# A decoder layer on one core: the mixture's base product moved ahead of the router's end, the last chunk's cross-attention in a list of its own, the experts' product transposed, and a bias added on GpSimd

## What is computed

```
x = LN(x + L0(x))          h = x + mamba(rms(x));  L0 = h + silu(rms(h) W1) * (rms(h) W2) W3
x = LN(x + xattn(x, ctx))  16 heads, 64 keys; the scores are scaled a second time by a
                           temperature made from their mean, max and entropy by a small MLP
x = LN(x + ffn(x))         x W + b + sum over e of gate[e] * (x A[e]) B[e]
                           gate: softmax over 8 experts, the top 2 kept and renormalised
```

## Time and profile before

| | |
|---|---|
| median of 3 runs | 4170.89 us (4154.61 to 4172.75) |
| the profiled execution | 4160.77 us |
| its span, first to last instruction | 4159.0 us |
| TensorE busy (matmuls) | 3674.8 us, 88% |
| DVE / ScalarE / GpSimd busy | 2519.4 / 2165.4 / 2441.5 us, 61 / 52 / 59% |
| mean granted TensorE clock | 0.938 of 2.4 GHz |
| moved by DMA | 483 MB, 116 GB/s on the mean |
| chain of work that ended last | TensorE 58%, GpSimd 7%, ScalarE 6%, DVE 6% |

### The profile page before, as it was taken

The page is one execution under the profiler, slowest core; times in us unless marked ns, Lnnn a source line. Parts: engine busy times, 40 slices in busy tenths (PEclk is TensorE's granted clock), DMA queues, the critical chain, the costliest instruction groups (busy, mean ns, idle before and its releaser), DMA issues.

```text
span 4159.0 us, 36287 instructions
## 1 busy us (share of the span) xinstructions
PE 3674.8 (88%) x9984; PEld 1760.8 (42%) x9984; DVE 2519.4 (61%) x3286; ACT 2165.4 (52%) x5182; POOL 2441.5 (59%) x1069
## 2 busy tenths in 40 slices
PE   7667998899879999999989998999989998999477
PEld 3223443444334445544434345554334434554244
DVE  4884678567746886168755887158774787222211
ACT  5543544554555455565456547455466457340543
POOL 3884599559954995049963997029981998100000
PEclk9889999899989999999989999999989999999788
DMA  4433344335433442235433442125432443112000
GB/s 171 138 121 101 120 164 162 97 115 167 149 106 117 158 156 74 86 112 168 152 111 104 157 159 97 66 83 187 152 128 82 157 162 119 49 46 91 11 31 21
DMA packets 221268, 483.19 MB, mean 116 GB/s; under 512 B 31884, under 2 KB 32268, under 8 KB 220812
## 3 DMA queue, kind: packets, MB, share of 16 engines
q1 hardware_dynamic: 221068, 480.87, 35.5%
HBM read 470.82 MB, written 9.96 MB: 116 GB/s over the span
## 4 chain that ended last, share of the span: by engine, by line
PE 58%; POOL 7%; ACT 6%; DVE 6%; issue 5%; POOLq 0%; DVEq 0%; ACTq 0%
PE ps L1542 32%; PE ps L1629 7%; PE ps L1644 6%; PE ps L1589 5%; POOL hb L1002 5%; DVE hb L1339 2%; POOL hb L992 2%; PE ps L1677 2%; PE ps L1711 1%; ACT ps L1220 1%; ACT xw L1254 1%; PE ps L1723 1%; PE ps L1582 1%; PE ps L1753 1%; PE ps L1740 1%
## 5 line engine op out<-in xcount | busy, mean ns | idle before, releaser
L1002 POOL TENSOR_TENSOR hb<-hb,bc 128x1024 f32<-128x1024 f32 x512 | 1224.5, 2394 | 96.8 <-issue 53.2
L992 POOL TENSOR_TENSOR hb<-dtu,bc 128x1024 f32<-128x1024 f32 x481 | 1133.2, 2357 | 124.3 <-PE ps L1644 85.6
L1049 ACT ACTIVATE ps<-dt,a_neg 128x512 f32<-128x512 f32 x1024 | 697.3, 690 | 841.1 <-DVE hb L1339 834.8
L1542 PE MATMUL ps<-fT,wden 128*128 128x512 f32 x2304 | 1038.5, 599 | 10.0 <-DVE hm L1392 6.7
L1644 PE MATMUL ps<-hb,ident 128*128 128x512 f32 x1152 | 653.2, 668 | 255.7 <-POOL hb L1002 254.3
L1542 PEld LDWEIGHTS ps<-fT,wden 128*128 128x128 f32 x2304 | 441.1, 193 | 568.4 <-issue 568.1
L1339 DVE TENSOR_TENSOR_SCAN hb<-ps,state,hb 128x512 f32<-128x512 f32 x512 | 626.6, 1266 | 19.2 <-POOL hb L992 12.9
L1339 DVE TENSOR_TENSOR_SCAN hb<-ps,hb 128x512 f32<-128x512 f32 x512 | 593.8, 1204 | 17.0 <-POOL hb L992 12.4
L1355 DVE TENSOR_TENSOR ps<-ps,hb 128x512 f32<-128x512 f32 x448 | 311.0, 694 | 274.1 <-POOL hb L1002 273.3
L1629 PE MATMUL ps<-wden,hm 128*128 128x512 f32 x1024 | 469.7, 606 | 1.5 <-DVE res L1402 1.5
L1542 PE MATMUL ps<-xnT,wmix 128*128 128x512 f32 x1024 | 456.9, 595 | 13.8 <-ACT xnT L1073 7.8
(11 more groups left out here) (197 smaller groups left out, 3980.5 us busy)
## 6 DMA issues: line engine op xcount, KB each, us to landing
bc<-bc_dram SPq DMA_DIRECT2D x1024, 256.0 KB, 3.6
wden<-in_w SPq DMA_DIRECT2D x192, 512.0 KB, 3.6
wmix<-in_w_mix SPq DMA_DIRECT2D x96, 512.0 KB, 3.7
watt<-in_w_qof SPq DMA_DIRECT2D x32, 512.0 KB, 4.3
xm<-in_x SPq DMA_DIRECT2D x8, 1024.0 KB, 5.5
res<-in_x SPq DMA_DIRECT2D x8, 1024.0 KB, 6.9
wden<-in_w_qof SPq DMA_DIRECT2D x16, 512.0 KB, 3.6
out<-res SPq DMA_DIRECT2D x8, 1024.0 KB, 4.3
```

Source lines behind the costliest of these rows:

```text
L992: TTn(hb[:, k % 4], dtu[:, :, :], bc[:, 0, k % 3].unsqueeze(1).broadcast_to([P, 2, CH]), ALU.mult).then_inc(s.s1_ready, 1)
L1002: TTn(hb[:, k % 4], hb[:, k % 4], bc[:, 1, k % 3].unsqueeze(1).broadcast_to([P, 2, CH]), ALU.mult).then_inc(s.s3_done, 1)
L1049: A_(dst, dt[:, p % 2, jj], ACT.Exp, scale=a_neg[:, j, n:n + 1]).then_inc(full_of(key), 1)
L1542: ins = M(dst, a, b, start=start and n == 0, stop=stop and n == len(pairs) - 1)
```

## The change

1. **Bias `bo` on GpSimd.** `wo` no longer has the product with `e64`. A new unit `bo` adds a broadcast tile `bo_b` to the four tiles of `res` on GpSimd, once the chunk's `turn` transposes have been read, in place: for chunk c - 1 behind `ht` of chunk c. `woa` waits for it.
2. **Experts' product transposed.** `hh` was 16 products of 128 columns (tokens as weights); now it is 4 of 512 with the expert matrix as weights. The gates are copied out to 128x512 (last operation of `top2`), transposed (`lora`) and copied by ScalarE, and `gh` multiplies there; `fin` waits for `gh`.
3. **Base products earlier.** One `base` stands ahead of `lora` in chunks 0 to 5, all four in chunks 6 and 7, whose last products then follow together.
4. **The last chunk's pass in its own list** (`w` beside `x`), which the planner may lay between units of chunk 6's pass. Waits between the two chunks' tiles are added for the shared buffers. Chunks 6 and 7 take base weights from `u`, free by then, and share the output weights in `watt`; chunk 6 keeps its gates in `hm`.
5. **One buffer for V.** `vbd` had two, now one; its load is a step of its own (`v_load`), behind the last `val` of the batch before.

```diff
-        got += [("hh", c), ("gh", c), ("lora", c), ("base", c, 0)]
+        early = 1 if c < CHUNKS - 2 else 4
+        got += [("hh", c)] + [("base", c, t) for t in range(early)] + [("lora", c), ("gh", c)]
         for t in range(TT):
-            got += [("fin", c, t), ("mixed", c, t)] + ([("base", c, t + 1)] if t + 1 < TT else [])
+            got += ([("base", c, t)] if t >= early else []) + [("fin", c, t), ("mixed", c, t)]
...
-    streams = {"m": m_plan(), "l": l_plan(), "x": x_plan(), "s": s_plan(), "y": y_plan()}
+    streams = {"m": m_plan(), "l": l_plan(), "x": x_plan(range(CHUNKS - 1)), "w": x_plan((CHUNKS - 1,)), "s": s_plan(), "y": y_plan()}
...
+            def load_v(b):
+                sp.wait_ge(s.zeroed, 2)
+                if b:
+                    filled(sp, ("val", 2 * b - 1, TT - 1))
...
+                elif kind == "bo":
+                    pool.wait_ge(s.const_in, 16 * CONSTS)
+                    for c4 in range(KC):
+                        filled(pool, ("tr", c, 0, c4))
+                    for t in range(TT):
+                        ins = TTn(res[:, c % 3, t], res[:, c % 3, t], bo_b[:, :], ALU.add)
+                    ins.then_inc(s.bo_in, 1)
...
+                    if q == 0 and i == 0 and c == CHUNKS - 1:
+                        filled(act, ("flip", c - 1, TT - 1, hf))
...
                 elif kind == "lora":
                     key = ("lora", c)
-                    A_(ghT, filled(act, key), ACT.Copy).then_inc(free_of(key), 1)
+                    A_(ghT_of(c), filled(act, key), ACT.Copy).then_inc(free_of(key), 1)
...
                     key = ("wo", c, i)
+                    dve.wait_ge(s.bo_in, c + 1)
...
-                        V.tensor_tensor(gates, G1, each(gmax[:, :]), ALU.mult).then_inc(free_of(("lg", c)), 1)
+                        ch.link(V.tensor_tensor(gates, G1, each(gmax[:, :]), ALU.mult))
+                        V.tensor_copy(gh_of(c).rearrange("p t (e r) -> p t e r", e=EXPERTS), bcast(gates, RANK)
+                                      ).then_inc(free_of(("lg", c)), 1)
...
-                    V.tensor_tensor(gh.rearrange("p t (e r) -> p t e r", e=EXPERTS), h, bcast(gate[:, 2], RANK), ALU.mult
-                                    ).then_inc(free_of(key), 1)
+                    V.tensor_tensor(ghT_of(c), filled(dve, key), ghT_of(c), ALU.mult).then_inc(free_of(key), 1)
...
-                    M(dst, e64[:, :], w_dt[:, 0:512], start=True, stop=False)
-                    group(dst, [(oT[:, c4 * P:(c4 + 1) * P], wo[c4 // 2][:, c4 % 2]) for c4 in range(KC)], start=False
-                          ).then_inc(full_of(unit), 1)
+                    group(dst, [(oT[:, c4 * P:(c4 + 1) * P], wo[c4 // 2][:, c4 % 2]) for c4 in range(KC)]).then_inc(full_of(unit), 1)
...
+                elif kind == "hh":
+                    group(take(pe, unit), [(w_ra[:, ci, EXPERTS:RA], qT[:, ci, half * CH:(half + 1) * CH]) for ci in range(KC)]
+                          ).then_inc(full_of(unit), 1)
```

More of the change, by code:

```diff
@@ L74, in m_plan @@
         got += scan(c) + end_and_front(c)
-    return got
+    return got + [("bo", CHUNKS - 1)]
 def l_plan():
@@ L120, in norm2, with x_plan @@
     return [("xvar", c, w, t) for t in range(TT)] + [("xrstd", c, w)] + [("xscale", c, w, t) for t in range(TT)]
-def x_plan():
+def x_plan(chunks):
     got = []
-    for c in range(CHUNKS):
+    for c in chunks:
         def e2(t, hf):
@@ L187, in m_parts @@
             part(ACT_, EV, mine(n))
+    elif kind == "bo":
+        part(POOL, 5.2, ("turn", c, KC - 1))
     elif kind == "out":
@@ L273, in parts @@
     elif kind == "xvar":
-        part(DVE, EV + 0.2, ("woa" if i == 1 else "mixed", c, u[3]))
+        part(DVE, EV + 0.2, ("woa" if i == 1 else "mixed", c, u[3]), ("xscale", c - 1, 2, last))
         if u[3] == last:
@@ L316, in parts @@
         part(PE, 0.65, ("e2", *key, 1), takes=(u,))
-        part(ACT_, EV, mine(), ("val", c, i - 1), gives=(u,))
+        part(ACT_, EV, mine(), ("val", c, i - 1) if i else ("val", c - 1, last), gives=(u,))
     elif kind == "val":
@@ L320, in parts @@
     elif kind == "on":
-        part(DVE, 1.0, ("val", *key), ("fl2", c, i - 1), gives=(("val", *key),))
+        part(DVE, 1.0, ("val", *key), ("fl2", c, i - 1) if i else ("fl2", c - 1, last), gives=(("val", *key),))
     elif kind == "fl2":
         part(PE, 0.65, ("on", *key), takes=(u,))
-        part(ACT_, EV, mine(), ("wo", c, i - 1), gives=(u,))
+        part(ACT_, EV, mine(), ("wo", c, i - 1) if i else ("wo", c - 1, last), gives=(u,))
     elif kind == "wo":
-        part(PE, 5 * MM, ("fl2", *key), takes=(u,))
+        part(PE, 4 * MM, ("fl2", *key), takes=(u,))
     elif kind == "woa":
-        part(DVE, EV, ("wo", *key), gives=(("wo", *key),))
+        part(DVE, EV, ("wo", *key), ("bo", c), gives=(("wo", *key),))
     elif kind in ("lg", "hh"):
-        part(PE, 2.5 if kind == "lg" else 3.5, ("xturn", c, last), takes=(u,))
+        part(PE, 3.6 if kind == "lg" else 4 * MM, ("xturn", c, last), takes=(u,))
     elif kind == "logits":
@@ L336, in parts @@
     elif kind == "gh":
-        part(DVE, EV, ("top2", c, 2), ("hh", c), gives=(("hh", c),))
+        part(DVE, EV, ("hh", c), ("lora", c), gives=(("hh", c),))
     elif kind == "lora":
-        part(PE, 0.65, ("gh", c), takes=(u,))
+        part(PE, 0.75, ("top2", c, 2), takes=(u,))
         part(ACT_, EV, mine(), gives=(u,))
@@ L343, in parts @@
     elif kind == "fin":
-        part(PE, MM, ("lora", c), ("base", *key))
+        part(PE, MM, ("gh", c), ("base", *key))
     elif kind == "mixed":
@@ L591, in loads @@
     got += [(kept, 2, ("kv_store", 0)), (kept + 4, 2, ("kv_load", 0)), (kept + 5, 2, ("kv_load", 1))]
+    got.append((kept + 6, 2, ("v_load", 0)))
+    for b in range(1, BATCH):
+        got.append((DONE[("val", 2 * b - 1, TT - 1)], 2, ("v_load", b)))
     for b in range(2, BATCH):
@@ L861, in load_wf @@
             def load_wf(c):
+                if c == CHUNKS - 2:
+                    filled(sp, ("out", CHUNKS - 1, TT - 1))
+                    for m in range(2):
+                        sp.dma_start(u[:, 2 * m:2 * m + 2].rearrange("p j l -> p (j l)"), A["w_qof"][4 + m]).then_inc(s.wu_in, 16)
+                    return
                 filled(sp, ("wo", c, TT - 1))
@@ L963, in _ @@
                     load_kv(c)
+                elif kind == "v_load":
+                    load_v(c)
                 elif kind == "store":
```

88 lines of the change are left out of this document (48 added, 40 removed).

## The result

| | before | changed |
|---|---|---|
| median of 9 runs each | 4167.2 us | 4189.7 us |
| range | 4154.6 to 4173.5 | 4175.8 to 4196.1 |
| profiled execution, span | 4159.0 | 4193.0 |

The changed kernel takes 1.0054 of the time before, 95% interval 1.0041 to 1.0066: slower by 0.54%, where the prediction said 4122 and faster. Busy time by stretch of the changed kernel, in the columns of the earlier trace rows: scan 3, gap 3, scan 4, gap 4, scan 7, gap 7, chunk 7's first attention, and the two last passes together.

What follows compares the result with a forecast made beforehand. TensorE was taken to bound the gaps, GpSimd's chain the scans, and neither TensorE nor ScalarE was full in the last two passes. Savings of 15 before 3941.3 and 28 after made 43: 4118 on the profiled scale, put at 4122, range 4088 to 4150.

Steps and rivals of the forecast that it cites:

- odd scans: Scans 3, 5 and 7: 0.4 of TensorE's relief credited, -2 us each, -6 together; bounds 0 and -15.
- gaps 3 and 5: Stretches after scans 3 and 5: -5.0 us of relief, but a 3.4 us feed-forward group comes forward, so -1.5 each.
- gaps 4 and 6: Stretches after scans 4 and 6: two 0.86 us score products go to the scan before, -1.7 us each.
- the experts' product: Router and experts' part of each pass: four 512-column products taken at 4.8 us for 6.3, saving 1.5 per pass.
- the bias: Output projection: one product fewer per tile's group, 3.5 us per pass off TensorE; GpSimd's additions of 5.1 costed at nothing.
- fills 4.3 us of TensorE: Base product 0, moved ahead of the gates' transposes, fills 4.3 us of TensorE; this moves work rather than removing it.
- three signs of being wrong: Odd scans past 345; ScalarE's gate-copy wait past 9 us in a scan; TensorE waiting over 25 between the last output projections.
- Gap 7: Stretch after the last scan, to 3861.8, 99% TensorE: shorter by 5 us.
- The end: From 3941.3, chunk 6's and 7's passes overlapped: -3 to pass 6's last projection, then 80 for 105.7, then +0.4; sum -28.
- Rival 2: Last two passes overlap poorly: TensorE's 11 us of waits become 27, the end gives -12, time 4148; chance 0.15.
- The rule against the change: DVE's gate copy in scans 3, 5, 7 may be held by GpSimd's port: 0.7 to 6.0 us each, 0.7 taken.
- Rival 4: Router's chain across engines delays scans: passes 0 to 5 each cost 5.4 + 6.0 us, about 4190, slower; chance 0.05.

Runs made afterwards that it cites:

- e12: Changed kernel, planner told chunks 0 to 5's output projection still takes five products, their early base product back at its old place: 4119.1 us, 0.9883.
- e6: e5 plus the transposed experts' product and its longer chain in passes 0 to 4, still in the old order: 4118.2 us, 0.9899.
- e5: e1 with the bias of passes 0 to 5 moved from TensorE to GpSimd, every engine's order of work kept: 4115.2 us, 0.9888.
- e3: Changed kernel with only the next chunk's first norm moved ahead of cross-attention's second variance root on ScalarE in scans 3 and 5: 4188.8 us, 1.0060.
- e1: Kernel before with the changed form for chunks 6 and 7 alone, passes 0 to 5 in the old form: 4138.9 us, 0.9945.
- e7: Same content as e5, but with the planner told of it, so that it writes all lists anew: 4153.0 us, 0.9978.

## Why the prediction was wrong

Content and order part well. e12 is 49 us under the kernel before (1.17%, interval 0.98 to 1.35), e6 42, e5 47; the sum was 43 and the forecast 4122. So the sum was near for a kernel that keeps the order. By stretch, e12 against the kernel before: odd scans -9.3 (forecast -6), gaps 3 and 5 -3.4 (-3), gaps 4 and 6 +1.0 (-3.4), from the last scan's end on -29.4 (-33). Part of this is luck: the experts' product, put at 1.5 a pass, gave nothing that shows, and the bias gave more than was credited. The order took back 71: by the ratios, 38 for the new lists that one number brings, most of it at the router's place (0.9962 to 1.0054), 22 for the lists around the planned early product, and 10, not clear of the intervals, for that product's place.

- **The step that failed** is "odd scans: I credit 0.4 of the relief, -2 each", with its bounds 0 and -15 that leave a loss out. Measured: +11.9, +15.1, +8.9. I had counted which stretch holds which pass and not at which step its in-order units stand. The third place of the order, shown ahead of the prediction, has two of the scan's sums (one in scan 7) moved behind the router and the base product; the prediction used that only for "fills 4.3 us of TensorE". What the runs showed in its place: router, experts' product and base product hold TensorE for 16.4 us ahead of sums 58 and 59, so GpSimd waits 9.47 us, and ScalarE's run of norms and copies holds DVE's next scan for 7.87. The price lay in rows too: 10.64 for router and experts' product, and steps of 4.7. In the old order e5, e6 and e12 have 336 to 343, the forecast's -2 or a little better. Of the prediction's three signs of being wrong this one came true (odd scans past 345); ScalarE's wait at the gate copy stayed at 8.2 to 8.6 in the odd scans.
- **Gaps.** "Gaps 3 and 5 -1.5 each, 4 and 6 -1.7 each" came out as +6.7, +1.9, +4.4 and +5.1. For gaps 4 and 6 it is the order: they take 109.8 to 110.2 in all five kernels whose planner knew of the early product, and 105.1 to 106.6 in the others. For gap 3 it need not be: e3, with the changed kernel's list on TensorE, has it at 179.8, at a granted clock of 0.97 (last section). In the old order gap 3 is 178.4 (e5) to 183.2 (e12) for 181.6, gap 5 181.5 to 182.6 for 186.4. Gap 7, forecast -5, was 308.1 for 308.0.
- **The experts' product.** Forecast -1.5 per pass. In the changed kernel router and experts' product take 12.2 and 13.2 us in passes 0 to 3 and 10.6 in the other four, against 9.1 to 13.3 before, so nothing or a loss. In e12, where the clock stayed up for most of it, they take 7.2 to 8.9 in five of eight. The size hangs on the clock of the moment; e6 and e12 against e5 show no gain that is clear of the noise.
- **The bias.** "At nothing" for GpSimd was right. Its relief of TensorE came through in full: 24 us of e5 against e1, give or take 10, where 3.5 times six passes is 21. The prediction let gaps and odd scans keep most of it.
- **The end.** Between the two last output projections 82.5 us (4053.3 to 4135.9) for a forecast of 80 and 105.7 before; TensorE waits 11.8 there for a forecast of about 11. Behind it +0.6 for +0.4. Rival 2 did not occur. Up to pass 6's last projection, gap 7's -5 and -3 were forecast, 8 together: -1.0 in the changed kernel, -8.0 in e6. TensorE in chunk 7's pass of the changed kernel, the third tile's wait (at 4118.44), behind pass 6's second normalisation on ScalarE, being the largest:

```profile
4047.59 5.73 PE L1577 MATMUL ps<-watt,xw 128*128 128x512 f32 x8 [0.75 <-ACT xw L1302]
...
4073.84 6.24 PE L1577 MATMUL ps<-qT,w_ra 128*128 128x512 f32 x8
...
4118.44 6.14 PE L1577 MATMUL ps<-watt,xw 128*128 128x512 f32 x8 [4.07 <-ACT xw L1302]
...
4130.73 5.12 PE L1577 MATMUL ps<-watt,xw 128*128 128x512 f32 x8 [0.75 <-ACT xw L1302]
```

- **The rule against the change.** By the Trainium skill (SBUF — State Buffer, "Who interferes with whom") the gate copy could have been held by GpSimd's port. No run here tests it: in no profile of this case was GpSimd at work during a gate copy, and the copy took 0.43 us each time. The price of nothing held, for a reason that the prediction did not give. Its own reason, that the median of the earlier trace rows is the least value, misread the row: of the 12 normalisation steps that start while GpSimd works, 9 took 0.73 to 6.03 us.
- **Rival 4** had the right place (chance 0.05, "about 4190") and half of the mechanism: exponentials of the scan behind the router's chain, base product 4.3 ahead. That its 4190 met the measured 4189.7 is luck: it added 11.4 to each of six passes, where three odd scans lost 9 to 15 each and gaps and lists the rest. e12 carries the whole longer chain and its copy at no cost that shows; it is the place of the chain and not its length. It should have been priced from the order: the group's time less what GpSimd can still do without the sums behind it. In scan 3 that is 16.4 us less the 8.1 in which GpSimd went on, and 1.2 from the sums' start to GpSimd's: the 9.5 measured.

## What to carry to other kernels

Where a planner writes in-order lists, one edit is two: the content, and every list that the new numbers bring. Put the content into the old lists first (fixed order), then replan, and time both; the lists can be compared without a run, which here led from lists that differ in some 460 places to one number. And a unit that feeds a ring needs its place read in steps: count what the moved group now stands ahead of, on all the engines that it crosses, and do not mend one engine's list alone.

The version to keep is e12 or e5: 4119 and 4115 us, 1.2 and 1.1% under the kernel before, 1.7% under the changed one.

## What the runs showed of the hardware

**The granted clock of a stretch was not fixed by its work.** Gap 3 of e3 has the changed kernel's list on TensorE, and TensorE's waits in it are the same in both, one by one (4.4, 1.1, 1.1, 0.9 us and so on). It took 179.84 us for 188.40, TensorE busy 168.76 for 177.32 us and idle for 11.1 in both, at a granted clock of 0.97 for 0.93:

```profile
1658.75:1838.59 179.84, 168.76 (x567) 89.67 (x566) 57.40 (x116) 97.72 (x320) 12.20 (x11) 0.97 0.22 71
```

e3's own gap 5, which holds the same units two chunks on, took 188.2 us at 0.93. So a gap that TensorE fills can come out 8.6 us longer or shorter through the clock alone, and the 5.5 us of busy time more in the changed kernel's gap 3 are no proof of a cost of the change. What makes the clock fall in one execution and not in the other stays open.

**What the lower level costs.** The eight records of the experts' product, always straight behind the router's, took 3.7 us in two passes of e12 at a granted clock of 1.00 over both products, 5.1 to 5.4 in three at 0.81, 6.2 and 6.5 in two at 0.68 and 6.5 in one at 0.53. The stretches at 1.2 GHz sum to 565 us in the profile of the changed kernel, to 513 before and to 476 in e12. Taking work off TensorE turned into its full time where the order kept the engine fed (e5), and not where it brought new waits (e7).
